# Broadcasting the local attention's weights from the 32 rows of each place, two places side by side

## The chip, the cores and the metric

The program runs on one core of a Trainium2 chip. The metric is the device time in microseconds (us); lower is better. TensorE (PE) multiplies, VectorE (DVE), ScalarE (ACT) and GpSimd (POOL) work on elements, SyncE (SP) issues the transfers. TensorE writes its results to PSUM, which the kernel uses as four "double banks" of 128 partitions x 2 x 512 numbers: `slot0`, `slot1`, `slot2` and `cps`. TensorE's work is shown in pairs: a weight load (PEld) puts the stationary operand into the array, a matmul (PE) streams the other operand through it.

## What is computed

For each of four images x (256 channels, 32 x 32 pixels):

```python
x = x + attention(group_norm(x))      # two halves of the channels, side by side:
#   window half: each 2x2 window of pixels attends to its own 4 pixels, 4 heads of 32
#     attn = softmax(q . k * SCALE over the 4 pixels m);  out[n] = sum_m attn[n, m] * v[m]
#   pooled half: all 1024 pixels attend to the 256 window means, 4 heads of 32
x = x + conv3x3(relu(group_norm(x) * mask)) + bias
```

The change touches the window half alone. There a pixel n has a weight for each of the four pixels ("places") m of its window and for each of the 4 heads. The weight of a head must be multiplied onto all 32 channels of that head.

## The kernel before, in words

The four images, b = 0 to 3, go through the same stages. The convolution of image b-1 is used as filling: its matmuls (288 an image, into `cps`) are handed out in small portions by `conv.more(n)` between the matmuls of the attention of image b, and each engine's order is written out by hand; queues run in that order and meet at semaphores. Image 0 has no older convolution to fill with.

The stage of the change is in `rest(b, ...)` of TensorE:

- `turned_weights` (L1389) turns the softmaxed window weights into `slot2`, with 128 rows: rows 32j to 32j+31 belong to place j. Of these 32 rows four hold the high part of the four heads' weights, four the low part; the others hold other data. ScalarE copies `slot2` to `p_w` (L608, fp32r, 128 x 1024 pixels) and signals `pt_act`.
- `values(j)` (L1396) broadcasts the weights of place j to the 128 channels: for each half of 512 pixels one matmul with the constant selector `sel[:, j]` (128 x 128, ones where a row is the high or low part of the column's head and of place j) and all 128 rows of `p_w`. It writes the double bank `value_bank(b, j)`: `slot0`, `slot1`, `slot0`, `slot2` for the four places (`PB_SLOT`), for image 0 `slot2` and `cps` in turns. Its end signals `pb_pe`. The helper `mm` that issues it is line L1113, so the profile shows these as "slot<-p_w,sel" at L1113.
- VectorE (its `step`, L986) multiplies each bank with the values of that place (`v_w`) into `pv[j]` and signals `pv_ready`; for images 2 and 3 it adds a finished quarter of the older convolution (`conv_result`, L889) between places 1 and 2. Two more additions (L994, L997) give the window output.
- TensorE puts filling between the places: `fill[3]` convolution matmuls after each place, 2 of them for image 1 (`REST_1`) and 3 for images 2 and 3 (`REST`). Place 2 writes `slot0` again, so TensorE waits for `pv_ready` of place 0 first.
- Then come the pooled half's last four score tiles (`pooled_scores`, i = 4 to 7, "slot<-qs,ks" at L1113, 98 rows), each of which needs its bank back (from `pv_ready` or from the exponentials `st_exp`). ScalarE takes the exponential of each (L563). When the last is done, `by_head` runs the pooled half's denominators and values: 128 x 32 column tiles, four heads side by side ("slot<-probs,cst" and "slot<-probs,lv").
- For image 0 there is no filling: each place is followed by one score tile (i = 3 to 6).

The selector comes in by a 256 KB transfer to `raw_sel` and is copied once by ScalarE to `sel` (L573).

Of the kernel before, what the change touches and what calls it, by code (L numbers as in the profile page):

```python
# [13 lines left out]
P = 128  # L14
# [29 lines left out]
C_IX = C_ONE + HD  # L44
C_IXR = C_IX + H
C_ALL = C_IXR + H
SEL_COLS = NW * P


WQ, WK, WV, WLQ, WLK, WLV = (P * i for i in range(6))  # L50
# [65 lines left out]
def build(nc, x, wqkv, whp, wlp, bh, bl, cw, cb, mw, filt, consts, selectors, out):  # L116
    with ExitStack() as ctx:
        def sb(name, shape, dt=F32):
            return ctx.enter_context(nc.sbuf_tensor(name, shape, dt))
# [4 lines left out]

        xy = sb("xy", [P, RING * KT * HW])
        cst = sb("cst", [P, C_ALL])
        sel = sb("sel", [P, NW, P], F32R)
        w_hi = sb("w_hi", [P, KT, WCOLS], F32R)
        w_lo = sb("w_lo", [P, KT, WCOLS], F32R)
        w_out = sb("w_out", [P, 2, P])  # L130
# [219 lines left out]
        def value_bank(b, j):  # L350

            return slot[PB_SLOT[j]] if b else (slot[2], cps)[j % 2]
# [93 lines left out]
        def _(act):  # L446
# [119 lines left out]
            def step(b, first, last):  # L566
                if first:
                    for cols, landed in zip(PIECES, w_in):
                        act.wait_ge(landed, KT * 16)
                        nc.scalar.copy(w_hi[:, :, cols], raw_w[:, :, cols]).then_inc(w_high, 1)  # L570
                    normalise_first()
                    act.wait_ge(c_in, CONST_LOADS)
                    nc.scalar.copy(sel[:].rearrange("p a b -> p (a b)"), raw_sel).then_inc(sel_act, 1)  # L573
                late = b + 1 == RING
                projections(b, first)
                if not first:
# [534 lines left out]
        def _(pe):  # L1111
            def mm(dst, lhsT, rhs, start, stop):
                return nc.tensor.matmul(dst, lhsT, rhs, start=start, stop=stop)  # L1113
# [267 lines left out]
            def rest(b, first, last):  # L1381
# [11 lines left out]
                                                  s_soft[:, n].rearrange("p j h -> p (j h)"), cst[:, C_ID:C_ID + P])  # L1393
                    ins.then_inc(pt_pe, 1)

                def values(j):  # L1396
                    for half in range(2):
                        ins = mm(value_bank(b, j)[:, half], sel[:, j], p_w[:, halves(half)], True, True)
                    ins.then_inc(pb_pe, 1)

                if first:
                    pe.wait_ge(sel_act, 1)
                    turned_weights()
                    scores(2)
                    pe.wait_ge(pt_act, b + 1)
                    for j in range(NW):
                        wait_count(pe, pv_ready, j - 1)
                        values(j)
                        scores(j + 3)
                    scores(LT - 1)  # L1410
                    pe.wait_ge(pv_ready, NW)
                else:
                    conv.more(fill[0])
                    for i in range(2, LT - NW):
                        scores(i)
                        conv.more(fill[1])
                    turned_weights()
                    conv.more(fill[2])
                    pe.wait_ge(pt_act, b + 1)
                    for j in range(NW):  # L1420
                        if j < 2:
                            pe.wait_ge(st_exp, b * LT + j + 3)
                        elif j == 2:
                            pe.wait_ge(pv_ready, b * NW + 1)
                        values(j)
                        conv.more(fill[3])
                    for i in range(LT - NW, LT):
                        if i < LT - 1:
                            pe.wait_ge(pv_ready, b * NW + i - 2)
                        else:  # L1430
                            pe.wait_ge(st_exp, b * LT + 5)
                        pooled_scores(b, i)
                        conv.more(fill[4])
# [54 lines left out]
def constants():  # L1488
# [6 lines left out]
    for h in range(HEADS):  # L1495
        c[:, C_HEAD + h] = p // HD == h
    c[:, C_ONE:C_ONE + HD] = 1
    for j in range(NW):
        for part in range(2):
            s[:, j * P:(j + 1) * P] += p[:, None] == HD * j + HEADS * part + p[None] // HD  # L1500
    c[:, C_IX:C_IX + H] = np.arange(1, H + 1)
    c[:, C_IXR:C_IXR + H] = np.arange(1, H + 1) + ROUND
    return c, s
# [30 lines left out]
```

## Time and profile before

| | |
|---|---|
| time, median of 3 runs | 350.07 us (350.04 to 353.92) |
| span of the profiled execution | 347.5 us |
| TensorE matmuls busy | 315.2 us, 91% of the span |
| VectorE busy | 272.5 us, 78% |
| ScalarE busy | 148.8 us, 43% |
| GpSimd busy | 83.0 us, 24% |
| chain that ended last | TensorE 58%, VectorE 23%, ScalarE 8% |
| mean granted TensorE clock | 0.979 of full speed |

"Busy" says only that an engine had work in hand. Which engine decides the time of a stage is read from the chain that ended last, and from the idle time in front of the instructions of the timeline. The ends of matmuls are modelled in this profile and overlap the next one's start; the distance from start to start is what a matmul costs in a row of them. A row of the timeline with "x2" merges two instructions: its duration runs from the first start to the last end.

### The profile page before, as it was taken

How to read it: one execution, taken by the hardware profiler on the slowest of the kernel's cores; microseconds unless marked ns; L12 is line 12 of the kernel's file. 1: busy time of each engine (PE TensorE's matmuls, PEld its weight loads, DVE VectorE, ACT ScalarE, POOL GpSimd, SP SyncE). 2: the span in 40 equal slices, each digit the busy share in tenths (PEclk: the TensorE clock that was granted, in tenths of full speed). 3: DMA queues.
4: the chain of work that ended last, by engine and by line, in shares of the span. 5: the costliest groups of instructions: out<-in, count | busy, mean ns of one | idle time of the engine just before them, and what ended most of it. 6: DMA issues, size and time to landing. Idle time of an engine off the chain costs nothing.

```text
span 347.5 us, 4162 instructions
## 1 busy us (share of the span) xinstructions
PE 315.2 (91%) x1566; PEld 222.3 (64%) x1566; DVE 272.5 (78%) x488; ACT 148.8 (43%) x189; POOL 83.0 (24%) x46
## 2 busy tenths in 40 slices
PE   0879968999979999999799999999799999999995
PEld 0566344267866663688567744888388727877884
DVE  4996668769999586889989767799887847897572
ACT  2442548464490843554047855351165423031300
POOL 2088513440436020003910200008600200202000
PEclk9999968899989999999999999999999999999999
DMA  8779500009700000099011200197001000101002
GB/s 276 276 102 140 228 5 0 2 1 134 94 0 4 2 1 2 0 130 159 1 63 41 82 1 2 35 128 128 4 0 62 0 0 5 58 0 62 0 0 121
DMA packets 12068, 20.38 MB, mean 59 GB/s; under 512 B 2065, under 2 KB 8081, under 8 KB 11793
## 3 DMA queue, kind: packets, MB, share of 16 engines
q1 hardware_dynamic: 12048, 20.13, 28.2%
q8 instruction: 12, 0.20, 0.2%
q14 instruction: 8, 0.06, 0.1%
HBM read 7.93 MB, written 4.19 MB: 35 GB/s over the span
## 4 chain that ended last, share of the span: by engine, by line
PE 58%; DVE 23%; ACT 8%; issue 6%; POOL 3%; DMA 2%; SPq 0%; DVEq 0%; POOLq 0%
PE slot L1113 29%; PE cps L1145 15%; PE slot L1189 7%; DVE l_max L848 3%; PE cps L1113 3%; DVE mask L784 3%; PE cps L1189 2%; ACT probs L563 2%; POOL probs L379 2%; DVE v_lo L814 1%; DMA xy<-x 1%; PE slot L1392 1%; ACT xn_hi L452 1%; ACT p_w L608 1%; DVE xn L740 1%
## 5 line engine op out<-in xcount | busy, mean ns | idle before, releaser
L1145 PE MATMUL cps<-v_hi,cw_hi 128*128 128x512 f32 (+1 forms) x144 | 57.6, 400 | 3.5 <-DVE v_lo L814 2.9
L1145 PE MATMUL cps<-v_hi,cw_lo 128*128 128x512 f32 (+1 forms) x144 | 57.9, 402 | 0.0
L1145 PE MATMUL cps<-v_lo,cw_hi 128*128 128x512 f32 (+1 forms) x144 | 56.4, 392 | 0.0
L379 POOL TENSOR_TENSOR probs<-q_w,k_w 128x1024 f32<-128x1024 f32 x14 | 32.9, 2376 | 79.5 <-DVE rw L777 72.3
L848 DVE TENSOR_REDUCE l_max<-slot 128x4 f32<-128x1024 f32 x32 | 37.1, 1216 | 5.9 <-PE slot L1113 5.9
L563 ACT ACTIVATE probs<-slot 128x1024 f32<-128x1024 f32 x32 | 31.4, 1021 | 16.0 <-PE slot L1113 15.9
L1145 PEld LDWEIGHTS cps<-v_hi,cw_hi 128*128 128x128 f32 x144 | 27.4, 191 | 12.7 <-issue 5.2
L1145 PEld LDWEIGHTS cps<-v_hi,cw_lo 128*128 128x128 f32 x144 | 27.4, 190 | 7.4 <-issue 2.2
L1145 PEld LDWEIGHTS cps<-v_lo,cw_hi 128*128 128x128 f32 x144 | 27.4, 190 | 5.0
L362 POOL TENSOR_TENSOR mask<-rw 128x1024 f32<-128x1024 f32 x8 | 15.2, 1912 | 56.6 <-DVE rw L777 56.6
L1113 PE MATMUL slot<-xn_hi,w_hi 128*128 128x512 f32 (+1 forms) x68 | 27.3, 401 | 1.1 <-ACT xn_hi L452 1.1
L1113 PE MATMUL slot<-xn_hi,w_lo 128*128 128x512 f32 (+1 forms) x68 | 26.1, 383 | 0.0
L1113 PE MATMUL slot<-xn_lo,w_hi 128*128 128x512 f32 (+1 forms) x68 | 25.9, 381 | 0.0
L546 ACT ACTIVATE xn<-mask 128x1024 f32<-128x1024 f32 x8 | 8.5, 1061 | 39.0 <-DVE mask L784 39.0
L557 ACT ACTIVATE v_hi<-mask 128x1024 fp32r<-128x1024 f32 x16 | 16.8, 1058 | 18.0 <-DVE mask L806 10.6
L1113 PE MATMUL slot<-probs,cst 128*32 128x512 f32 x176 | 23.1, 638 | 0.0
L1113 PE MATMUL slot<-qs,ks 98*128 98x512 f32 x64 | 21.4, 428 | 1.7 <-DMA qs<-probs 1.7
L1113 PEld LDWEIGHTS slot<-ks,qs 96*128 96x128 f32 x128 | 18.2, 194 | 6.3 <-DVE l_max L848 3.8
L814 DVE SCALAR_TENSOR_TENSOR v_lo<-mask,v_hi 128x1024 fp32r<-128x1024 f32 x16 | 19.2, 1220 | 3.6 <-ACT v_hi L557 3.6
L1113 PE MATMUL slot<-ks,qs 96*128 96x256 f32 x128 | 20.3, 293 | 1.2 <-DVE l_max L848 0.8
L427 POOL TENSOR_TENSOR q_w<-q_w,k_w 128x1024 f32<-128x1024 f32 x3 | 7.3, 2419 | 56.8 <-DVE k_w L986 56.8
L532 ACT ACTIVATE xn<-xy,gn 128x1024 f32<-128x1024 f32 x8 | 9.6, 1239 | 17.2 <-DVE gn L679 17.2
(197 smaller groups left out, 635.0 us busy)
## 6 DMA issues: line engine op xcount, KB each, us to landing
xy<-x SPq DMA_DIRECT2D x8, 512.0 KB, 6.6
out<-xy SPq DMA_DIRECT2D x8, 512.0 KB, 2.6
qs<-probs SPq DMA_DIRECT2D x12, 256.0 KB, 5.8
qs<-probs SPq DMA_DIRECT2D x24, 128.0 KB, 8.3
raw_cw<-conv_w SPq DMA_DIRECT2D x2, 1152.0 KB, 6.4
ks<-probs SPq DMA_DIRECT2D x12, 128.0 KB, 6.9
probs<-h_qkv SPq DMA_DIRECT2D x2, 192.0 KB, 3.8
probs<-l_kv SPq DMA_DIRECT2D x2, 128.0 KB, 3.7
```

What stands on the lines that cost most here:

```text
L362: nc.gpsimd.tensor_tensor(mask[:, k].rearrange("p (h w) -> p h w", h=H), rw[:, k, 0].unsqueeze(2).to_broadcast([P, H, W]), rw[:, k, 1].uns ...
L379: nc.gpsimd.tensor_tensor(product(b, j).rearrange("p (n w) -> p n w", n=NW), q_w[:].rearrange("p (n w) -> p n w", n=NW), k_w[:, j * G:(j + ...
L532: nc.scalar.activation(xn[:, k], img(b, k), ACT.Identity, bias=gn[1][:, 6, k:k + 1], scale=gn[1][:, 5, k:k + 1]).then_inc(yn_ready, 1)
L546: nc.scalar.activation(xn[:, k], mask[:, k], ACT.Relu).then_inc(relu, 1)
L557: nc.scalar.activation(v_hi[:, k, 2 * phase:2 * phase + 2].rearrange("p a b -> p (a b)"), mask[:, k], ACT.Copy, scale=TILE_SCALE[phase]).t ...
L563: nc.scalar.activation(probs[:, i], flat[score_slot(b, i)], ACT.Exp, scale=SCALE / NW)\
L784: nc.vector.scalar_tensor_tensor(mask[:, k], mask[:, k], -1.0, xn[:, k], ALU.max, ALU.mult).then_inc(masked, 1)
L814: nc.vector.scalar_tensor_tensor(v_lo[:, k, part].rearrange("p a b -> p (a b)"), mask[:, k], TILE_SCALE[phase], v_hi[:, k, part].rearrange ...
L848: nc.vector.tensor_reduce(l_max[:, bass.ds(n, HEADS, step=NB)], flat[LA_SLOT[n]].rearrange("p (h m) -> p h m", h=HEADS), AX_X, ALU.max, ne ...
L1113: return nc.tensor.matmul(dst, lhsT, rhs, start=start, stop=stop)
L1145: ins = nc.tensor.matmul(cps[:, pos % 2, y0 * WT:y1 * WT], (cw_hi, cw_hi, cw_lo)[part][:, k, pos, dy + 1, o * P:(o + 1) * P], (v_hi, v_lo, ...
L1189: ins = nc.tensor.matmul(last_bank(o, pos)[:, y0 * WT:y1 * WT], (cw_hi, cw_hi, cw_lo)[part][:, k, pos, dy + 1, o * P:(o + 1) * P], (v_hi, ...
```

## The change

The selector becomes one 128 x 128 matrix: row p is one for the columns of its head, by its place among 32 (the same in each of the four blocks of 32 rows). A broadcast of place j now reads the 32 rows 32j to 32j+31 of the selector and of `p_w` alone. The program gives such a matmul a tile of 32 rows x 128 columns of the array, at row 32j; before, all of these matmuls had the whole 128 x 128 array. The products and the banks stay as they were; only which rows are read changes.

For images 1 to 3, `values` takes two places: half 0 of the first, half 0 of the second, half 1 of the first, half 1 of the second. The two places stand in neighbouring row tiles and write to different double banks (`slot0` and `slot1`, then `slot0` and `slot2`). The filling that stood behind each place stands behind each pair (twice as many matmuls). The wait of place 1 for the exponential of score tile 3 now stands ahead of the first pair. For image 0 each place is still alone.

The selector's transfer and ScalarE's copy of it become a quarter (64 KB, 128 x 128).

```diff
--- before.py
+++ after.py
@@ -44,7 +44,7 @@
 C_IX = C_ONE + HD
 C_IXR = C_IX + H
 C_ALL = C_IXR + H
-SEL_COLS = NW * P
+SEL_COLS = P
 
 
 WQ, WK, WV, WLQ, WLK, WLV = (P * i for i in range(6))
@@ -124,7 +124,7 @@
 
         xy = sb("xy", [P, RING * KT * HW])
         cst = sb("cst", [P, C_ALL])
-        sel = sb("sel", [P, NW, P], F32R)
+        sel = sb("sel", [P, P], F32R)
         w_hi = sb("w_hi", [P, KT, WCOLS], F32R)
         w_lo = sb("w_lo", [P, KT, WCOLS], F32R)
         w_out = sb("w_out", [P, 2, P])
@@ -570,7 +570,7 @@
                         nc.scalar.copy(w_hi[:, :, cols], raw_w[:, :, cols]).then_inc(w_high, 1)
                     normalise_first()
                     act.wait_ge(c_in, CONST_LOADS)
-                    nc.scalar.copy(sel[:].rearrange("p a b -> p (a b)"), raw_sel).then_inc(sel_act, 1)
+                    nc.scalar.copy(sel[:], raw_sel).then_inc(sel_act, 1)
                 late = b + 1 == RING
                 projections(b, first)
                 if not first:
@@ -1393,10 +1393,14 @@
                                                   s_soft[:, n].rearrange("p j h -> p (j h)"), cst[:, C_ID:C_ID + P])
                     ins.then_inc(pt_pe, 1)
 
-                def values(j):
+                def values(places):
+
                     for half in range(2):
-                        ins = mm(value_bank(b, j)[:, half], sel[:, j], p_w[:, halves(half)], True, True)
-                    ins.then_inc(pb_pe, 1)
+                        for j in places:
+                            rows = slice(HD * j, HD * (j + 1))
+                            ins = mm(value_bank(b, j)[:, half], sel[rows], p_w[rows, halves(half)], True, True)
+                            if half == 1:
+                                ins.then_inc(pb_pe, 1)
 
                 if first:
                     pe.wait_ge(sel_act, 1)
@@ -1405,7 +1409,7 @@
                     pe.wait_ge(pt_act, b + 1)
                     for j in range(NW):
                         wait_count(pe, pv_ready, j - 1)
-                        values(j)
+                        values((j,))
                         scores(j + 3)
                     scores(LT - 1)
                     pe.wait_ge(pv_ready, NW)
@@ -1417,13 +1421,12 @@
                     turned_weights()
                     conv.more(fill[2])
                     pe.wait_ge(pt_act, b + 1)
-                    for j in range(NW):
-                        if j < 2:
-                            pe.wait_ge(st_exp, b * LT + j + 3)
-                        elif j == 2:
-                            pe.wait_ge(pv_ready, b * NW + 1)
-                        values(j)
-                        conv.more(fill[3])
+                    pe.wait_ge(st_exp, b * LT + 4)
+                    values((0, 1))
+                    conv.more(2 * fill[3])
+                    pe.wait_ge(pv_ready, b * NW + 1)
+                    values((2, 3))
+                    conv.more(2 * fill[3])
                     for i in range(LT - NW, LT):
                         if i < LT - 1:
                             pe.wait_ge(pv_ready, b * NW + i - 2)
@@ -1495,9 +1498,8 @@
     for h in range(HEADS):
         c[:, C_HEAD + h] = p // HD == h
     c[:, C_ONE:C_ONE + HD] = 1
-    for j in range(NW):
-        for part in range(2):
-            s[:, j * P:(j + 1) * P] += p[:, None] == HD * j + HEADS * part + p[None] // HD
+    for part in range(2):
+        s += p[:, None] % HD == HEADS * part + p[None] // HD
     c[:, C_IX:C_IX + H] = np.arange(1, H + 1)
     c[:, C_IXR:C_IXR + H] = np.arange(1, H + 1) + ROUND
     return c, s
```

TensorE, image 1, from the first broadcast to the first of the last four score tiles. The names are double banks written and tiles read; "x2" is two instructions of one kind in a row. Before:

```order
L1113 MATMUL slot0<-p_w,sel 128x512 x2
L1145 MATMUL cps<-v_lo,cw_hi 128x496
L1145 MATMUL cps<-v_hi,cw_lo 128x496
L1113 MATMUL slot1<-p_w,sel 128x512 x2
L1145 MATMUL cps<-v_hi,cw_hi 128x512
L1145 MATMUL cps<-v_lo,cw_hi 128x512
L1113 MATMUL slot0<-p_w,sel 128x512 x2
L1145 MATMUL cps<-v_hi,cw_lo 128x512
L1145 MATMUL cps<-v_hi,cw_hi 128x512
L1113 MATMUL slot2<-p_w,sel 128x512 x2
```

After, the same stretch, up to the second pair's last broadcast:

```order
L1113 MATMUL slot0<-p_w,sel 128x512
L1113 MATMUL slot1<-p_w,sel 128x512
L1113 MATMUL slot0<-p_w,sel 128x512
L1113 MATMUL slot1<-p_w,sel 128x512
L1145 MATMUL cps<-v_lo,cw_hi 128x496
L1145 MATMUL cps<-v_hi,cw_lo 128x496
L1145 MATMUL cps<-v_hi,cw_hi 128x512
L1145 MATMUL cps<-v_lo,cw_hi 128x512
L1113 MATMUL slot0<-p_w,sel 128x512
L1113 MATMUL slot2<-p_w,sel 128x512
L1113 MATMUL slot0<-p_w,sel 128x512
L1113 MATMUL slot2<-p_w,sel 128x512
```

The eight broadcasts stand in two groups of four, with four convolution matmuls between the groups where two stood between places; the last four of the filling, two of which stood ahead of place 3, follow the second group. The second group holds the wait for VectorE's product of place 0.

TensorE, image 2, the second half of the same stage. Before:

```order
L1113 MATMUL slot0<-p_w,sel 128x512 x2
L1145 MATMUL cps<-v_hi,cw_lo 128x496
L1145 MATMUL cps<-v_hi,cw_hi 128x496
L1145 MATMUL cps<-v_lo,cw_hi 128x496
L1113 MATMUL slot2<-p_w,sel 128x512 x2
L1145 MATMUL cps<-v_hi,cw_lo 128x496
L1145 MATMUL cps<-v_hi,cw_hi 128x512
L1145 MATMUL cps<-v_lo,cw_hi 128x512
L1113 MATMUL slot1<-qs,ks 128x512 x2
```

After:

```order
L1113 MATMUL slot0<-p_w,sel 128x512
L1113 MATMUL slot2<-p_w,sel 128x512
L1113 MATMUL slot0<-p_w,sel 128x512
L1113 MATMUL slot2<-p_w,sel 128x512
L1145 MATMUL cps<-v_hi,cw_lo 128x496
L1145 MATMUL cps<-v_hi,cw_hi 128x496
L1145 MATMUL cps<-v_lo,cw_hi 128x496
L1145 MATMUL cps<-v_hi,cw_lo 128x496
L1145 MATMUL cps<-v_hi,cw_hi 128x512
L1145 MATMUL cps<-v_lo,cw_hi 128x512
L1113 MATMUL slot1<-qs,ks 128x512 x2
```

The score tile that follows has the same six convolution matmuls and the same four broadcasts ahead of it, in another order. Image 3 reads as image 2. VectorE's order is the same in both kernels.

## Rows read from the trace of the kernel before

**Rows 1.** The page: span, busy time of TensorE, chain that ended last

```profile
span 347.5 us, 4162 instructions
PE 315.2 (91%) x1566; PEld 222.3 (64%) x1566; DVE 272.5 (78%) x488; ACT 148.8 (43%) x189; POOL 83.0 (24%) x46
PE 58%; DVE 23%; ACT 8%; issue 6%; POOL 3%; DMA 2%; SPq 0%; DVEq 0%; POOLq 0%
```

**Rows 2.** Instructions on `sel`: durations in ns (min/median/max), first and last start

```profile
L1113 PE MATMUL slot<-p_w,sel x28: 388/396/796, 52.1 to 271.1; 128*128 128x512 f32 x28
L573 ACT CAST sel<-probs x1: 603/603/603, 14.2 to 14.2; 128x512 fp32r<-128x512 f32 x1
```

**Rows 3.** Stages: stretch, length, busy of each engine, TensorE clock, DMA

```profile
121.70:130.20 8.50, 7.84 (x32) 5.88 (x32) 7.64 (x7) 3.79 (x4) 2.41 (x1) 1.00 0.00 1
192.60:203.20 10.60, 10.32 (x45) 8.22 (x45) 8.40 (x8) 8.39 (x13) 2.42 (x1) 1.00 0.14 50
267.30:277.90 10.60, 10.39 (x46) 8.24 (x45) 8.41 (x8) 4.11 (x4) 2.42 (x1) 1.00 0.00 0
```

**Rows 4.** Chain that ended last: start, us, what; selector copy, images 1, 2, 3

```profile
14.29 1.22 DVE xn_lo L706
...
126.40 3.79 ACT probs L563 x4
...
192.65 0.74 PE slot L1113 x2
...
202.10 1.04 ACT probs L563
...
276.77 1.04 ACT probs L563
```

**Rows 5.** Timeline, image 1: start, us, engine, line, operation, idle before it

```profile
121.74 0.72 PE L1113 MATMUL slot<-p_w,sel 128*128 128x512 f32 x2 [0.65 <-ACT p_w L608]
...
122.49 1.23 DVE L986 TENSOR_TENSOR q_w<-slot,v_w 128x1024 f32<-128x1024 f32 x1 [3.01 <-PE slot L1113]
...
123.77 0.74 PE L1113 MATMUL slot<-p_w,sel 128*128 128x512 f32 x2
...
125.74 0.62 PE L1113 MATMUL slot<-qs,ks 98*128 98x512 f32 x2
```

**Rows 6.** Timeline, image 2: product of place 0, score tile 4, its exponential

```profile
193.43 1.23 DVE L986 TENSOR_TENSOR q_w<-slot,v_w 128x1024 f32<-128x1024 f32 x1 [1.78 <-PE slot L1113]
...
197.33 0.63 PE L1113 MATMUL slot<-qs,ks 98*128 98x512 f32 x2
...
198.06 1.03 ACT L563 ACTIVATE probs<-slot 128x1024 f32<-128x1024 f32 x1 [0.60 <-PE slot L1113]
```

**Rows 7.** Timeline of TensorE around column tiles (128*32) and turns (L1392)

```profile
108.91 0.39 PE L1145 MATMUL cps<-v_hi,cw_lo 128*128 128x496 f32 x1
...
109.23 2.95 PE L1113 MATMUL slot<-probs,cst 128*32 128x512 f32 x16
...
112.11 0.49 PE L1145 MATMUL cps<-v_hi,cw_hi 128*128 128x496 f32 x1
...
112.44 0.38 PE L1145 MATMUL cps<-v_lo,cw_hi 128*128 128x496 f32 x1
...
119.54 1.09 PE L1392 MATMUL slot<-cst,k_w 128*128 128x128 f32 x8 [0.31 <-DVE k_w L876]
...
130.55 3.64 PE L1113 MATMUL slot<-probs,cst 128*32 128x512 f32 x32
134.12 1.98 PE L1113 MATMUL slot<-k_w,w_out 128*128 128x512 f32 x4
```

**Rows 8.** Timeline, image 0: broadcast 0, exponentials, denominators

```profile
52.08 1.22 PE L1113 MATMUL slot<-p_w,sel 128*128 128x512 f32 x2 [0.25 <-ACT p_w L608]
...
53.84 5.08 ACT L563 ACTIVATE probs<-slot 128x1024 f32<-128x1024 f32 x5 [0.89 <-PE slot L1113]
...
59.30 5.34 PE L1113 MATMUL slot<-probs,cst 128*32 128x512 f32 x32
```

## The prediction

> **What bounds the kernel now.** I read the page first. The span is 347.5 us, TensorE's matmuls fill 91% of it, and the chain that ended last runs over TensorE for 58% of the span and over VectorE for 23% [rows 1]. So a saved TensorE microsecond is worth something on a good half of the way, and only there. The chain, then the timeline, tell for the stage of the change. I compare the sum with the profiled execution; it is 2.57 us shorter than the median of 350.07 us, and I take that difference as unchanged.
>
> The table by stages shows the broadcasts' stretches of images 1, 2 and 3, 8.5, 10.6 and 10.6 us long, with TensorE busy 7.84, 10.32 and 10.39 us of them at the full granted clock of 1.00 [rows 3]. In images 2 and 3 the chain enters on a broadcast (192.65) and leaves by one exponential alone, of score tile 7 (202.10 and 276.77) [rows 4]. In between TensorE runs without a gap, and ScalarE waits for it: 0.60 us ahead of the exponential of tile 4 [rows 6]. Here each TensorE instruction taken away counts. In image 1 the filling is shorter, and the chain leaves by four exponentials in a row, 126.40 to 130.19 [rows 4]: TensorE counts only until score tile 4 is written, 125.74 plus 0.62 [rows 5]. Image 0 is bound by five exponentials in a row from 53.84 on, after ScalarE waited 0.89 us for TensorE [rows 8].
>
> **What one broadcast costs.** There are 32 of them; the 28 into `slot` have a median of 396 ns [rows 2], but that is a modelled duration. Two in a row take 0.63 us like the two of a score tile [rows 6], so one follows another after 0.63 - 0.40 = 0.23 us. After a wait it is 0.72 - 0.39 = 0.33 us [rows 5]: a restart costs 0.10 us. A convolution matmul costs 0.23 us too (108.91 and its neighbours are of the same kind, [rows 7]); the filling between groups is then 4 x 0.23 = 0.91 us in image 1 and 6 x 0.228 = 1.37 us in images 2 and 3.
>
> **Do row tiles run side by side?** No matmul of the kernel before has 32 rows, so the trace bounds this from the nearest rows. One end is the column tiles: 32 matmuls of the denominators, four tiles in turn, take 3.64 us, 0.11 us each, while four of the same type on the whole array take 1.98 us, close to 0.5 us each [rows 7]. Four tiles of the array do run together there. The other end is that two row tiles do not overlap, 0.23 us for each as now. What could bring it between them is the weight load: here each matmul loads 128 columns, the column tiles only 32. The turns give a ceiling on that: eight matmuls of 128 columns, each with its own load of 128 columns, take 1.09 us; leaving out the last one's 0.27, that is 0.12 us a load [rows 7]. Four loads then need 0.47 us, about what two overlapped pairs of matmuls need (2 x 0.23). So loads may delay the second place of a group by 0.12 us but not undo the overlap. I take the middle of "both at once" and "0.12 us late", since the operands differ from the column tiles in just this.
>
> The Trainium skill (TensorE: Matmul & The Clock Gate, Part 3, packing small matmuls) says that one matmul with 32 rows costs as much as one with 128 and that only tiles with different row groups bring a gain, the next one starting about 4 ns after the first; no run here shows that for rows yet. By it the sum would be at its fast end, 1.41 us.
>
> **The price of changing tiles.** From the last convolution matmul at 108.91 to the first column tile at 109.23 are 0.32 us instead of 0.23, and after the column tiles the second convolution matmul comes 0.33 us after the first (112.11, 112.44) [rows 7]. That is 0.10 us for each change of tiling. A group that starts after a wait already holds the 0.10. So the group of four, from its first broadcast to the first convolution matmul behind it: 0.33 (half 0 of both places) + 0.23 (half 1) + 0.10 (back) = 0.66 us; with late loads 0.78.
>
> The Trainium skill (TensorEngine Tiling (Array Packing), Key Properties) holds that a change of tiling mode drains the engine, which speaks against this change, with 20 more such changes in the program (two for each of the six groups and four single places). A drain would show at least the tail by which a matmul's modelled duration exceeds its step, some 0.17 us, not 0.10; by that the sum would be 0.4 us smaller. The rows at 109.23 and 112.44 show 0.10.
>
> **The sum.**
> - Image 1. Now from 121.74 to score tile 4 at 125.74, 4.00 us. After: 0.66 + 0.91 brings TensorE to 123.31. There it must wait for the product of place 0. That starts when half 1 of place 0 is done, as now at 122.49, and ends at 123.72; the broadcast of place 2 starts at 123.77 as it does now [rows 5]. Then 0.66 + 0.91: score tile 4 at 125.34, **0.40 us earlier**. 0.46 us of what was saved in the first group goes into this wait. ScalarE's four exponentials start that much earlier; score tile 6 waits for the product of place 3 and comes just in time.
> - Image 2. Now 192.65 to 197.33, 4.68 us. After: 0.66 + 1.37 brings it to 194.68; the product of place 0 ends at 193.43 + 1.23 = 194.66 [rows 6], so the second group starts at about 194.72. With 0.66 + 1.37 score tile 4 stands at 196.75, **0.58 us earlier**. ScalarE's idle 0.60 us is just enough to take it.
> - Image 3 has the same instructions in the same order and a stretch of the same 10.6 us, with TensorE even fuller [rows 3]; the same working gives **0.58 us earlier**.
> - Image 0. Places are alone, so nothing overlaps, and each costs two changes of tiling. Those behind place 0 delay score tile 3 and with it the five exponentials; the clock is still low there (the first broadcast pair takes 1.22 us instead of 0.72 [rows 8]). One change at 0.10 to 0.20: **0.15 us later**. The other places have more than 0.2 us to spare before VectorE wants them.
> - The selector: ScalarE's copy of 0.60 us at 14.2 [rows 2] becomes some 0.2 to 0.3, but the chain is on VectorE's split then (14.29) [rows 4], and ScalarE next waits for TensorE. **Nothing.** Were the cover gone, it would be 0.4 us. The smaller transfer is equally behind other work.
> - The wait for the exponential of tile 3, now ahead of place 0, costs nothing: ScalarE copies `p_w` after that exponential, and the broadcasts need `p_w` anyway.
>
> Together 0.40 + 0.58 + 0.58 - 0.15 = 1.41 us less if row tiles start together. With loads 0.12 us late in each of six groups it is 0.7 less, 0.7. The middle is 1.05 us: **349.0 us**. Everything behind the last exponential of an image (the column tiles, projections, the next image's front) hangs on it, so I let the gain pass whole.
>
> **The rivals.**
> - *Row tiles do not overlap* (the price of a change then decides): a group costs 0.33 + 3 x 0.23 + 0.10 = 1.12 us, and place 0 is ready 0.23 us later, since its half 1 is third in line. Image 1: 123.77, product at 123.95, second group at 124.00, score tile 4 at 126.03: 0.29 later. Image 2: 192.65 + 2 x (1.12 + 1.37) = 197.63, 0.30 later, and image 3 as much. With image 0 that is 1.0 us slower: 351.1. For it: no 32-row tile in the trace, and `p_w` and `sel` are fp32r, which the column tiles are not. Against it: the column tiles' 0.11 us. It decides from the point where the second place starts more than 0.15 us after the first. Chance 0.15.
> - *The clock falls once more.* The denominators of image 0 took 5.34 us in a stretch with the low clock level instead of 3.64 [rows 7, 8]: 1.7 us for one such stretch. It follows short idle stretches of TensorE; this change makes one more short wait in images 1 to 3 and uses a quarter of the rows. With the gain taken off: 349.0 + 1.7 = 350.7; with no overlap 352.8. Against it: the clock was 1.00 in all three stretches [rows 3], with waits of 0.65 us in them. Chance 0.08.
> - *The saved time is absorbed*: TensorE arrives earlier but something else is late, so the gain turns into waits for VectorE's products (places 2 and 3) or into idle time later. Then 350.0 to 350.3. For it: 0.46 us in image 1 is lost so already, and in image 2 ScalarE has no more than 0.02 us left. Against: images 2 and 3 leave by a single exponential that waits for TensorE. Chance 0.07.
> - My forecast has the remaining 0.70.
>
> **How the numbers follow.** The forecast's own range runs from 348.0 (together, and no price for changing tiles: 6 x 0.10 more than 1.41) to 349.5 (loads late and a quarter microsecond lost on the way). The whole range takes in absorption and the case without overlap, and leaves out the fast edge and most of the low clock's case: 347.8 to 351.3. Two per cent, about what a measurement of this kernel can tell from no change, are 7 us; the whole stage's broadcasts together, 24 x 0.23 = 5.5 us, are less. So within 2% in every case: 0.98, and 0.01 on either side.
>
> **What would show it.** In the timeline of the changed kernel, image 2: the four broadcasts of a group within about 0.33 us from first to last start, the next convolution matmul 0.33 us behind the last; a short wait of the second group for `q_w` L986 in image 1 (0.4 to 0.5 us); the distance from the first broadcast to score tile 4 at 3.6 us in image 1 (now 4.00) and 4.1 us in images 2 and 3 (now 4.68). I am wrong if the starts within a group are 0.23 us apart, if the stretches of [rows 3] show a clock below 1.00, or if the first matmul of a group or behind it is later by more than 0.2 us.

## The result and the profile after

The changed kernel takes **354.33 us** (median of 4 runs, 354.0 to 356.14) against 351.81 us of the kernel before (4 runs, 350.04 to 353.92). The ratio is 1.0138 with a 95% interval of 1.0086 to 1.0189: slower, by 1.4%. Ratios and intervals leave out the runs more than 1.5% above the fastest of their kernel, which the medians and ranges keep, so a ratio need not be the quotient of the two medians. In a second comparison (6 runs against 17) it was 354.77 against 350.19 us, 1.0147 (1.0101 to 1.0194). I had forecast 349.0 us and a range up to 351.3; only the 0.98 for "within 2%" came true.

The page of the changed kernel, to be held against [rows 1]; the row PEclk is the granted TensorE clock in tenths, in 40 slices of 8.8 us:

```profile
span 351.7 us, 4162 instructions
PE 319.8 (91%) x1566; PEld 220.0 (63%) x1566; DVE 272.9 (78%) x488; ACT 148.3 (42%) x189; POOL 82.9 (24%) x46
...
PEclk9989986599999999999999999999999999999999
...
PE 56%; DVE 22%; ACT 7%; issue 6%; POOL 5%; DMA 2%; SPq 0%; DVEq 0%; POOLq 0%
```

The span is 4.2 us longer. TensorE is busy 4.6 us more although 24 of its 32 broadcasts now run two at a time. The clock row gives the place: slices 7 and 8, that is 53 to 70 us, image 0.

The instructions on `sel`, as in [rows 2] (ns, min/median/max):

```profile
L1113 PE MATMUL slot<-p_w,sel x28: 383/490/791, 53.0 to 274.3; 32*128 32x512 f32 x28
...
L573 ACT CAST sel<-probs x1: 289/289/289, 13.8 to 13.8; 128x128 fp32r<-128x128 f32 x1
```

The stages of images 1 to 3, as in [rows 3] (stretch, length, busy of PE, PEld, DVE, ACT, POOL, clock, DMA share, GB/s):

```profile
126.70:134.90 8.20, 7.38 (x32) 4.93 (x32) 7.35 (x7) 3.77 (x4) 2.41 (x1) 1.00 0.00 1
...
197.40:207.60 10.20, 10.01 (x44) 7.22 (x44) 8.39 (x8) 8.24 (x12) 2.42 (x1) 1.00 0.17 54
...
271.70:281.90 10.20, 10.05 (x45) 7.22 (x44) 8.39 (x8) 4.11 (x4) 2.42 (x1) 1.00 0.00 0
```

All three are shorter, 8.2 for 8.5 and 10.2 for 10.6 us, at a clock of 1.00. The timeline of image 1 shows how, and answers to [rows 5]:

```profile
126.73 0.73 PE L1113 MATMUL slot<-p_w,sel 32*128 32x512 f32 x4 [0.65 <-ACT p_w L608]
127.39 0.49 PE L1145 MATMUL cps<-v_lo,cw_hi 128*128 128x496 f32 x1
127.48 1.23 DVE L986 TENSOR_TENSOR q_w<-slot,v_w 128x1024 f32<-128x1024 f32 x1 [3.00 <-PE slot L1113]
...
127.72 0.38 PE L1145 MATMUL cps<-v_hi,cw_lo 128*128 128x496 f32 x1
...
128.76 0.73 PE L1113 MATMUL slot<-p_w,sel 32*128 32x512 f32 x4 [0.19 <-DVE q_w L986]
...
130.46 0.64 PE L1113 MATMUL slot<-qs,ks 98*128 98x512 f32 x2
```

Four broadcasts now fit into the 0.73 us that two took. The last of them starts 0.33 us after the first, so the second place of a pair starts with the first and no weight load holds it up. The first convolution matmul stands 0.66 us behind the group's start, to the hundredth what I had worked out; but the next comes only 0.33 us later, not 0.23. Score tile 4 is reached after 3.73 us instead of 4.00, and in image 2 after 4.35 instead of 4.68. That the row tiles run side by side agrees with the Trainium skill (TensorE: Matmul & The Clock Gate, Part 3).

What happened in image 0 is seen in its timeline, to be held against [rows 8]:

```profile
52.96 0.73 PE L1113 MATMUL slot<-p_w,sel 32*128 32x512 f32 x2 [0.64 <-ACT p_w L608]
53.62 0.73 PE L1113 MATMUL slot<-qs,ks 98*128 98x512 f32 x2
...
54.94 1.22 PE L1113 MATMUL slot<-qs,ks 98*128 98x512 f32 x2
...
57.23 1.22 PE L1113 MATMUL slot<-qs,ks 98*128 98x512 f32 x2
...
62.83 0.56 PE L1113 MATMUL slot<-mv,cst 128*128 128x4 f32 x2 [1.22 <-issue]
```

At first two broadcasts and two score matmuls alternate every 0.66 us, where two of the whole array cost 0.46. From 55 us on they take 1.15 us each: the clock has gone to its lower level. It stays there, by the table in steps of 4 us (the number behind the brackets is the clock; before, then after):

```profile
50.00:54.00 4.00, 3.75 (x13) 0.59 0.00 0
54.00:58.00 4.00, 3.67 (x14) 1.00 0.00 0
58.00:62.00 4.00, 2.99 (x21) 0.76 0.00 0
62.00:66.00 4.00, 4.00 (x24) 0.81 0.01 4
66.00:70.00 4.00, 4.00 (x34) 1.00 0.00 0
```

```profile
50.00:54.00 4.00, 3.36 (x15) 0.80 0.00 0
54.00:58.00 4.00, 4.00 (x10) 0.62 0.00 0
58.00:62.00 4.00, 3.61 (x8) 0.50 0.00 0
62.00:66.00 4.00, 3.17 (x18) 0.50 0.00 0
66.00:70.00 4.00, 4.00 (x25) 0.67 0.01 4
```

The denominators, 32 matmuls that take 3.64 us at full clock [rows 7], fall into it whole (6.25 us). But most of theirs did so before, too (5.34 us, [rows 8]).

**Where the 4.2 us are.** Between the first broadcasts of two images the two timelines read 52.08, 121.74, 192.65, 267.28 and the end at 347.5 before, and 52.96, 126.73, 197.42, 271.74 and 351.7 after. So 0.88 us were lost ahead of image 0's broadcasts, 4.11 us from there to image 1's, and 0.22, 0.31 and about 0.26 us were won in the three parts behind.

The 0.88 us lie in the projections of image 0, where the changed kernel's profile has a low clock from 20 to 24 us and that of before has none. That looks like chance: a later profile of the changed kernel has 1.00 there, and one of a kernel with the front of the kernel before has 0.58. The 4.11 us are what the experiments are about.

### The profile page after: what moved, and what is told of

It reads as the page before. It is cut to its first block, busy times and chain, and to the rows that moved or that the text cites. A ratio compares the mean times of both kernels' runs of the same rounds, so it can differ in the third digit from the quotient of the medians.

```text
span 351.7 us, 4162 instructions
## 1 busy us (share of the span) xinstructions
PE 319.8 (91%) x1566; PEld 220.0 (63%) x1566; DVE 272.9 (78%) x488; ACT 148.3 (42%) x189; POOL 82.9 (24%) x46
## 4 chain that ended last, share of the span: by engine, by line
PE 56%; DVE 22%; ACT 7%; issue 6%; POOL 5%; DMA 2%; SPq 0%; DVEq 0%; POOLq 0%
PE slot L1113 29%; PE cps L1145 12%; PE slot L1189 7%; POOL probs L379 5%; PE cps L1113 3%; DVE l_max L848 3%; DVE mask L784 3%; PE cps L1189 2%; ACT probs L563 2%; DVE v_lo L814 2%; PE slot L1392 1%; DMA xy<-x 1%; ACT xn_hi L452 1%; ACT p_w L608 1%; DVE xn L740 1%
## 5 line engine op out<-in xcount | busy, mean ns | idle before, releaser
L1113 PE MATMUL slot<-probs,cst 128*32 128x512 f32 x176 | 24.9, 661 | 0.1
L557 ACT ACTIVATE v_hi<-mask 128x1024 fp32r<-128x1024 f32 x16 | 16.8, 1058 | 18.0 <-DVE mask L806 10.6
L1113 PE MATMUL slot<-qs,ks 98*128 98x512 f32 x64 | 22.8, 455 | 1.8 <-DMA qs<-probs 1.8
```

Source lines behind the costliest of these rows:

```text
L557: nc.scalar.activation(v_hi[:, k, 2 * phase:2 * phase + 2].rearrange("p a b -> p (a b)"), mask[:, k], ACT.Copy, scale=TILE_SCALE[phase]).t ...
```

## The experiments

Three theories: single row tiles in image 0 use too few rows, and the clock falls for it; the changes of tiling, with the pauses they bring, make it fall; or it falls by chance. Each ratio is against the kernel before on the same chip, with its 95% interval.

### The changed kernel again

> The changed kernel again, beside the kernel before and the three below on one chip. Two theories. A, rows: the eight single broadcasts of image 0, of 32 rows each, leave TensorE's array so little used that the granted clock falls to its lower level in this stage (48 to 69 us), whatever the run; it costs 3 to 5 us, of which the pairs of images 1 to 3 give back 1.0 us (8.50, 10.60 and 10.60 us became 8.2, 10.2 and 10.2). B, chance: the low stretches of the clock fall here or there from run to run in either kernel, and the changed kernel's runs so far had more of them by luck. A expects a ratio of 1.005 to 1.015 against the kernel before with the granted clock low from about 55 to 68 us again; B expects 0.995 to 1.003 and a clock that differs from run to run.

354.77 us against 350.19, ratio 1.0147 (1.0101 to 1.0194), as theory A had it. The kernel before ran from 347.89 to 354.32 us with mean clocks from 0.985 down to 0.961, the changed one from 351.57 to 356.36 with 0.976 to 0.952. So the clock does differ from run to run in both; but the changed kernel lies lower as a whole. Its profile has the low stretch in the same place (0.50 from 54 to 66 us). Chance explains the spread, not the shift.

### Image 0 on the whole array, pairs in images 1 to 3

```diff
+                def pairs(places):
+                    for half in range(2):
+                        for j in places:
+                            rows = slice(HD * j, HD * (j + 1))
+                            ins = mm(value_bank(b, j)[:, half], sel[rows, j], p_w[rows, halves(half)], True, True)
...
-                        values(j)
-                        conv.more(fill[3])
+                    pairs((0, 1))
+                    conv.more(2 * fill[3])
```

The large selector stays and image 0 keeps `values(j)` of the kernel before.

> Images 1 to 3 as in the changed kernel (pairs of row tiles), image 0 as before (all 128 rows, whole array); the selector is the large one, so its transfer and copy are as before. Theory A (rows of image 0): the low clock of 55 to 68 us is gone, and what is left is the gain of images 1 to 3, 1.0 us less than the kernel before, ratio 0.997. Theory B (chance): like the changed kernel of the same call. If the pairs themselves cost clock somewhere, this one stays slower than the kernel before.

350.16 us, ratio 0.9995 (0.9962 to 1.0029). The whole loss is gone, so it is image 0's. Its mean clocks, 0.966 to 0.985, lie where those of the kernel before do (0.961 to 0.985), so the pairs show no cost in clock. I had expected 0.997; whether the pairs' 1.0 us comes out at the end this run cannot tell: the interval reaches from 0.3% to either side.

### Image 0 in row tiles, images 1 to 3 as before

```diff
                 def values(j):
+                    rows = slice(HD * j, HD * (j + 1)) if first else slice(0, P)
                     for half in range(2):
-                        ins = mm(value_bank(b, j)[:, half], sel[:, j], p_w[:, halves(half)], True, True)
+                        ins = mm(value_bank(b, j)[:, half], sel[rows, j], p_w[rows, halves(half)], True, True)
```

> The other half alone: image 0 with single 32-row broadcasts, images 1 to 3 with the whole array as before, large selector. Theory A: the full loss without the gain, 3 to 5 us more than the kernel before (ratio 1.010 to 1.014), and a low clock from about 55 to 68 us in the trace. Theory B: within 0.3 us of the kernel before apart from the changes of tiling, which cost 0.15 to 0.5 us.

354.75 us, 1.0147 (1.0101 to 1.0192): the other half alone has the whole loss, at the upper end of what theory A expected. With the large selector in both halves, the smaller transfer and copy are out as a cause too. Its clock in image 0:

```profile
50.00:54.00 4.00, 3.30 (x9) 0.82 0.00 0
54.00:58.00 4.00, 4.00 (x8) 0.50 0.00 0
58.00:62.00 4.00, 2.78 (x14) 0.50 0.00 0
62.00:66.00 4.00, 4.00 (x24) 0.50 0.02 4
66.00:70.00 4.00, 4.00 (x28) 0.98 0.00 0
```

### 64 rows instead of 32

```diff
-                    rows = slice(HD * j, HD * (j + 1)) if first else slice(0, P)
+                    rows = slice(2 * HD * (j // 2), 2 * HD * (j // 2 + 1)) if first else slice(0, P)
```

> As the previous one, but each broadcast of image 0 reads 64 rows (its own 32 and its neighbour's, for which the selector holds zeros): tiles of 64 rows x 128 columns, just as many changes of tiling as with 32 rows, twice the rows in use. If the rows in use decide the clock, this lies between: a shorter low stretch or none, 0 to 2 us more than the kernel before. If the pauses from the changes of tiling decide it, it is as slow as with 32 rows, 3 to 5 us more.

355.59 us, 1.0165 (1.0131 to 1.0199). Twice the rows, and no better. This speaks against the number of rows and for the changes of tiling, which are the same eight, or for something else that the two have in common: both are row tiles.

### All 128 rows, but the changes of tiling

```diff
                 def values(j):
+                    if first:
+                        mm(value_bank(b, j)[0:HD, 0, 0:1], cst[:, C_ONE:C_ONE + HD], cst[:, 0:1], True, True)
                     for half in range(2):
```

> The kernel before, with one thing added: ahead of each of image 0's four broadcasts TensorE does one column of a 128 x 32 column tile into the bank that the broadcast then overwrites. That makes the same eight changes of tiling as in the changed kernel, while the broadcasts keep all 128 rows. The 32-row and the 64-row version were equally slow (1.0147 and 1.0165), so I now expect that the pauses at the changes of tiling, not the rows in use, let the clock fall: then this is slow too, ratio 1.008 to 1.016, with a low clock until 66 to 68 us. If the rows in use decide it, only the changes themselves cost, 0.5 to 1 us, ratio 1.001 to 1.003, with the clock as in the kernel before.

354.04 us (12 runs, 350.77 to 355.25), 1.0100 (1.0063 to 1.0138). One column of a column tile ahead of each broadcast, 128 rows in use everywhere, and the kernel is slow: it needs neither fewer rows nor row tiles. The added matmul (two instructions in the trace) stands 0.20 us ahead of the broadcasts, and the pause before it is no wait for another engine:

```profile
54.82 1.05 PE L1113 MATMUL slot<-qs,ks 98*128 98x512 f32 x2
55.81 0.27 PE L1113 MATMUL cps<-cst 128*32 128x1 f32 x2
56.01 1.22 PE L1113 MATMUL cps<-p_w,sel 128*128 128x512 f32 x2
57.02 1.05 PE L1113 MATMUL slot<-qs,ks 98*128 98x512 f32 x2
```

The clock was 0.50 from 50 to 62 us in this profile. It was low before the first added matmul (53.61 us), as in the kernel before at that point, so this profile does not show a change of tiling bringing it down. It shows two things in one: at the low clock a place with its score tile takes 2.20 us (54.82 to 57.02), where the kernel with image 0 on the whole array takes 1.70 (54.41 to 56.11 in its profile), and the low clock lasts until 62 us instead of 58. How the 3.8 us divide between the price itself and a clock that is low for longer, the run leaves open; the mean clock of its 12 runs is 0.969, of the 24 of the kernel before 0.978. Of the 12 runs three were at 350.8 us. Whether the fewer rows add something (1.0147 against 1.0100) is left open, as the intervals overlap.

### Image 0 in pairs too

```diff
-                    for j in range(NW):
-                        wait_count(pe, pv_ready, j - 1)
-                        values((j,))
-                        scores(j + 3)
-                    scores(LT - 1)
+                    values((0, 1))
+                    scores(3)
+                    scores(4)
+                    pe.wait_ge(pv_ready, 2)
+                    values((2, 3))
+                    for i in range(5, LT):
+                        scores(i)
```

> The changed kernel with image 0 in pairs too: places 0 and 1, score tiles 3 and 4, then places 2 and 3, score tiles 5 to 7. Half the changes of tiling (four instead of eight) and half the array time. If the pauses decide the clock, the stretch is denser in one way and shorter in another; I expect some of the loss back, ratio 1.003 to 1.010. If rows in use decide it, TensorE is now less used than with single places, and it stays at 1.013 or more.

354.06 us, 1.0107 (1.0063 to 1.0152). Half the changes take back at most a part; the number lies just beyond the upper end of what I expected, and cannot be told from the changed kernel's. Nor is it a clean test of the changes, for this order has a wait of its own: the second pair needs VectorE's product of place 1, and TensorE stands still for it at full clock.

```profile
58.02 0.49 PE L1113 MATMUL slot<-p_w,sel 32*128 32x512 f32 x1 [1.32 <-DVE k_w L986]
```

### TensorE kept at work in image 0

```diff
                 ins.then_inc(stok_pe, 1)
                 if first:
+                    keep_warm(3, slot[2][:, 1])
...
                     scores(2)
+                    keep_warm(1)
                     pe.wait_ge(pt_act, b + 1)
...
                     pe.wait_ge(pv_ready, NW)
+                    keep_warm(1)
```

The five matmuls, each of which is two instructions in the trace, write to banks that are free then. First into the changed kernel:

> The changed kernel with TensorE kept at work where it waits in image 0: three more matmuls of 384 columns on constants while it waits for the maxima's transfer (about 45.5 to 47.2 us), one while it waits for p_w, one ahead of its wait for the last exponentials. Nothing reads their results. If the clock carries the whole loss, it stays high through image 0's denominators and the ratio falls from 1.015 to 0.99 or 1.00. If the changed tiles cost time by themselves in image 0, the ratio stays above 1.008.

352.29 us (12 runs, 347.96 to 354.01), 1.0038 (1.0004 to 1.0072). Then into the kernel before:

> The same five matmuls in the kernel before, as the control. The kernel before has its own low stretches in image 0 (0.76 mean clock from 47 to 60 us, 0.5 from 60 to 63), so I expect it to gain 1 to 3 us, ratio 0.991 to 0.997. The difference to the previous kernel is then what the change is worth with the clock out of play: by the stages of images 1 to 3, 1.0 us in favour of the change, less some 0.7 us for image 0's changes of tiling.

347.65 us (346.25 to 348.02), 0.9913 (0.9882 to 0.9944). I had set 0.99 or 1.00 for the changed kernel if the clock carried the whole loss, and above 1.008 if the tiles cost time by themselves; it came out between, and it stays 4.6 us above its control. But its profiled run, of 349.00 us, gives a clean measurement, since the clock is 1.00 through image 0 in both. The changed kernel, then the control:

```profile
52.03 0.73 PE L1113 MATMUL slot<-p_w,sel 32*128 32x512 f32 x2 [0.33 <-ACT p_w L608]
52.69 0.73 PE L1113 MATMUL slot<-qs,ks 98*128 98x512 f32 x2
53.35 0.73 PE L1113 MATMUL cps<-p_w,sel 32*128 32x512 f32 x2
...
59.42 0.39 PE L1113 MATMUL slot<-mv,cst 128*128 128x4 f32 x2 [0.46 <-ACT probs L563]
```

```profile
52.27 0.73 PE L1113 MATMUL slot<-p_w,sel 128*128 128x512 f32 x2 [0.34 <-ACT p_w L608]
52.83 0.62 PE L1113 MATMUL slot<-qs,ks 98*128 98x512 f32 x2
53.29 0.62 PE L1113 MATMUL cps<-p_w,sel 128*128 128x512 f32 x2
...
58.67 0.39 PE L1113 MATMUL slot<-mv,cst 128*128 128x4 f32 x2
```

From the first broadcast to the group means are 7.39 against 6.40 us: **image 0's changes of tiling cost 0.99 us by themselves**, at full clock.

The changed kernel with the five matmuls again:

> The changed kernel with the five constant matmuls again. Its runs fell into two groups (348 to 349 and 352 to 353.5 us) and the profile showed a fast one, with the clock at 1.00 through image 0. Here I want the trace of the slower group. If the changes of tiling still let the clock fall there, a low stretch lies between 55 and 68 us; if something else makes them slow, the clock is 1.00 there and the time is lost elsewhere.

352.83 us, 1.0045 (0.9984 to 1.0106). The profiled run took 353.04 us and shows the fall itself:

```profile
51.09 0.81 PE L1113 MATMUL cps<-cst 128*128 128x384 f32 x2
52.23 0.73 PE L1113 MATMUL slot<-p_w,sel 32*128 32x512 f32 x2 [0.33 <-ACT p_w L608]
52.89 0.73 PE L1113 MATMUL slot<-qs,ks 98*128 98x512 f32 x2
53.55 0.73 PE L1113 MATMUL cps<-p_w,sel 32*128 32x512 f32 x2
54.21 0.73 PE L1113 MATMUL slot<-qs,ks 98*128 98x512 f32 x2
54.87 1.06 PE L1113 MATMUL slot<-p_w,sel 32*128 32x512 f32 x2
55.86 1.22 PE L1113 MATMUL slot<-qs,ks 98*128 98x512 f32 x2
...
61.93 5.30 PE L1113 MATMUL slot<-probs,cst 128*32 128x512 f32 x32
```

From 28 to 54.9 us the clock is full, and from 45.7 us on TensorE has waited for nobody longer than 0.33 us. After four groups in alternating tilings it is halved, and the denominators need 5.30 us. The control has the same waits (0.84 us up to 45.7 in both, then 0.33 and 0.34) and no such fall. So this fall needs no idle stretch that the control does not have as well; what the kernel has besides is the alternation. It does not always suffice: of the changed kernel's 21 runs with the five matmuls 17 have a mean clock of 0.971 or less and four 0.980, and the profile of one of these four has no fall in image 0. Of the 31 runs with the five matmuls and image 0 on the whole array, those of the next section included, none is below 0.975. Whether it is the pauses or the 32 rows of every second group, this pair of kernels cannot tell; that the rows are not needed rests on the two runs with 64 and 128 rows.

### The version that the runs point to

The five matmuls, with the pairs in images 1 to 3 and image 0 on the whole array, beside the control again:

> The kernel before with the five constant matmuls in image 0 once more, beside the next one on the same chip: 0.991 of the kernel before again, with the clock at 1.00 through image 0.

> The same with the pairs of row tiles in images 1 to 3, image 0 on the whole array. With the clock out of play in image 0, this shows what the pairs are worth: if the stages read from the profile (0.3, 0.4 and 0.4 us shorter) come through to the end, 1.0 us less than the previous kernel, ratio to the kernel before 0.988. If the gain is absorbed behind those stages, the same as the previous kernel within 0.3 us.

347.76 us, 0.9961 (0.9928 to 0.9994), and 347.61 us, 0.9941 (0.9902 to 0.9980). I had expected 0.991 and 0.988. The control itself moved from 0.9913 to 0.9961 between two comparisons, so the difference of 0.15 us is below what these runs resolve.

The traces tell more. In these two profiles the clock also falls in places that I had not looked at, around 170 and 245 us, between the stages; in the control's first profile it does not. From the first broadcasts of images 1 and 2 to those of the next image the control takes 71.59 and 75.33 us with these falls, 70.91 and 74.65 without them: 0.68 us each. "The clock out of play" thus holds for image 0 alone. Both kernels have these two falls, so they can be compared: from image 0's first broadcast to the last matmul the control takes 290.44 us and the kernel with pairs 289.47. The pairs' gain does come through, 0.97 us in this pair of profiles; the changed kernel's first profile with the five matmuls has the same two falls and takes 290.51 us.

With three more such matmuls where TensorE waits for the first convolution's operands in image 1:

```diff
                     elif starting and n == 5:
                         weights_ready()
+                        keep_warm(3)
```

> Pairs in images 1 to 3, image 0 on the whole array, the five constant matmuls, and three more where TensorE waits for the first convolution's operands in image 1 (about 97.6 to 99.7 us, after which most traces show 0.5 of full clock until 104). If that low stretch is what is left, 0.5 to 1 us less than with five, ratio 0.985 and a mean clock of 0.998.

347.48 us, 0.9925 (0.9888 to 0.9962). I had expected 0.985 and a mean clock of 0.998; the mean clocks are 0.980 to 0.995, and the gain over the previous kernel cannot be told from nothing. Its profile has a clock of 1.00 from 96 to 110 us, but so has the control's first profile, and that stretch was not what was left: the control takes 67.50 us from image 0's first broadcast to image 1's with this fall and 67.52 without it, and the falls around 170 and 245 us are still there (289.72 us from the first broadcast to the last matmul). Its median is the lowest of the study, 2.7 us below the kernel before (350.16), and its interval lies below 1; it cannot be told from the control, which has 2.4 of the 2.7 us without any row tile. So most of it is the clock, not the broadcasts.

## Why the prediction was wrong, point by point

- **TensorE counts in images 1 to 3: right.** The stage from the first broadcast to what follows the last exponential took 8.50, 10.54 and 10.57 us in every profile with whole-array broadcasts, to 0.03 us, and 8.23, 10.21 and 10.21 in every one with pairs. In the first comparison 0.22, 0.31 and 0.26 us of that reached the next image or the end, so "I let the gain pass whole" was nearly right.
- **Row tiles side by side: right,** and at the fast end. The late weight loads, for which I had taken off 0.36 us, did not show. The rival without overlap is out.
- **The price of changing tiles: half its size.** I had read 0.10 us from 108.91 to 109.23 and 0.10 us from 112.11 to 112.44 and charged each change 0.10 once. But these are two parts of a price: 0.10 us ahead of the first matmul of the new tiling and 0.10 more behind it. In the changed kernel both stand behind one change (0.66 with 0.10 in it, then 0.33), and in image 2 0.10 more ahead of the second group, which follows a convolution matmul after 0.32 us. A change costs 0.20 us. The images' gains came out as 0.27, 0.33 and 0.36 us instead of 0.40, 0.58 and 0.58. The Trainium skill (TensorEngine Tiling (Array Packing), Key Properties) has the engine drain at each change of tiling mode; the 0.20 us fit that better than my 0.10.
- **Image 0: the term that was mis-sized.** I counted one change of eight, 0.15 us, since only score tile 3 seemed to be waited for. In truth TensorE takes the chain over: a broadcast group and a score group of 0.66 us each make 1.32 us for a score tile, and ScalarE, with exponentials of 1.02 us, then waits 0.30 us for each. Before, five of them ran in a row [rows 8]. With the constant matmuls, at full clock, the timeline of ScalarE has, in the changed kernel and then in the control

```profile
54.78 1.02 ACT L563 ACTIVATE probs<-slot 128x1024 f32<-128x1024 f32 x1 [0.30 <-PE slot L1113]
...
56.11 1.02 ACT L563 ACTIVATE probs<-slot 128x1024 f32<-128x1024 f32 x1 [0.30 <-PE slot L1113]
...
57.43 1.94 ACT L563 ACTIVATE probs<-slot 128x1024 f32<-128x1024 f32 x2 [0.30 <-PE slot L1113]
```

```profile
53.49 5.13 ACT L563 ACTIVATE probs<-slot 128x1024 f32<-128x1024 f32 x5 [0.35 <-PE slot L1113]
```

  The first exponential starts 1.43 us behind the first broadcast instead of 1.22, and the fourth 3.97 us behind the first (53.46 to 57.43) instead of 3.19 (53.49 to 56.68): 0.21 and 0.78 are the 0.99 us. With it and the gains as measured, the change is worth 0.0 us at full clock: 0.96 won, 0.99 lost. The two profiles with the same low stretches behind image 0 agree: 290.51 us against 290.44 from the first broadcast to the last matmul.
- **The clock: the step that failed.** I had a fall of the clock as a rival, but with a chance of 0.08, put at nothing in the sum, with one stretch of 1.7 us, and in the wrong place. I looked for it in the stages of images 1 to 3, whose clock was 1.00, and in idle stretches and the number of rows. It was in image 0, where the rows already showed the clock at its lower level around the denominators [rows 8]. From the first broadcast of image 0 to that of image 1 the profiles give 67.5 us for a whole-array kernel with full clock, 69.66 for the kernel before, 68.49 for the changed one with full clock and 73.77 for the changed one as it is. So the clock cost the kernel before 2.1 us there and the changed kernel 5.3. Those 3.1 us more, with the 0.99 us, are the 4.11 us of the first section. Most of the 3.1 us lie in the stage itself and not, as my rival had it, in the denominators: from the first broadcast to the denominators the changed kernel takes 10.36 us, 7.70 at full clock, and the kernel before 7.22 and 6.71, which is 2.15 us more for the clock; the denominators take 6.18 and 5.26 us from their start to the next matmul's (3.58 at full clock), 0.92 us more. All this is read from one profile of each kernel. That the clock falls is measured; that the changes of tiling bring it down rests on the comparisons above, and why they do is not shown.
- **My range** ended at 351.3 because each case moved by itself. The direct loss and the clock go together here: the changes that lengthen image 0 are those with which the clock fell, and the longer stage then runs slowly.
- **My signs of being wrong** did not warn. The starts within a group were not 0.23 us apart, the stages had a clock of 1.00, the first matmul behind a group was on time (0.66 us); the short wait for `q_w` in image 1 was there, with 0.19 us instead of 0.4 to 0.5. The distances to score tile 4, 3.73 and 4.35 us for 3.6 and 4.1, pointed at the price of a change alone. All of them looked at images 1 to 3, and none at image 0.

## What to carry to other kernels

Packing small matmuls into row tiles pays where several tiles go in one group and the group stands in dense filling: four broadcasts in the time of two, less 0.20 us for each change of tiling. A single small tile between whole-array matmuls gains nothing, pays two changes, and in a stretch without filling the clock came down with it, in most runs, for this stretch and the work behind it. Before a change adds pauses to TensorE, look up the granted clock of that very stage over several runs: where the clock falls, the stage itself and what follows it run at half clock (here 2.15 us in the stage and 0.92 us in the 32 matmuls behind it), and that is the price, not the pause. And a stretch like image 0, where TensorE has no filling, deserves a sign of being wrong of its own.

## What the runs showed that I had not expected

- The granted clock fell from its upper level (2.4 GHz) to the lower (1.2 GHz) with TensorE waiting no longer than 0.33 us for another engine in the 9 us before, after four groups that alternated between 32-row tiles and the whole array (54.9 us in the changed kernel with five constant matmuls). One column of a column tile ahead of each broadcast group made the kernel slower too, with all 128 rows in use (1.0100); how much of that is the clock is open.
- Runs of one program differ by 2%, and the time goes with the mean clock: of the kernel before ten runs at 0.985 have a mean of 347.99 us, six at 0.975 one of 350.20 and two at 0.961 one of 354.00 (one comparison, 34 runs).
- The clock also fell between the stages of images 1 to 3, around 170 and 245 us, in some profiles and not in others of the same kernel, for 0.68 us each.
- Five matmuls whose results nobody reads made the kernel before faster, 0.9913 and 0.9961 in two comparisons.
